# A decoder's first self-attention on one core: VectorE scales queries and keys in one operation, ScalarE spreads the keys

## The chip, the cores and the metric

The kernel runs on one core of a Trainium2 chip. The metric is the device time of one execution, in microseconds. Five instruction streams run side by side and meet only at semaphores: PE (TensorE), DVE (VectorE), ACT (ScalarE), POOL (GpSimd) and SP (SyncE, which here only issues transfers). An engine runs its own instructions strictly in the order in which they are written; a wait holds everything behind it on that engine.

## The reference, cut to what matters

Two decoder layers, each of attention, cross-attention and a feed-forward part with a layer norm after each, over 32 sequences of 64 tokens with 256 features. The change lies in the first attention alone:

```python
q = (x @ Wq + bq).reshape(B, T, N_HEAD, hd)      # 16 heads of 16
k = (x @ Wk + bk).reshape(B, T, N_GROUPS, hd)    # 4 groups of 16
v = (x @ Wv + bv).reshape(B, T, N_GROUPS, hd)
k = jnp.repeat(k, KV_PER_HEAD, axis=1)           # each group serves 4 heads
v = jnp.repeat(v, KV_PER_HEAD, axis=1)
q_hat = q / (norm(q) + EPS)
k_hat = k / (norm(k) + EPS)
q_r = apply_rope(q_hat * alpha * sqrt(hd), cos, sin)
k_r = apply_rope(k_hat, cos, sin)
attn = softmax(where(causal, q_r @ k_r.T / sqrt(hd), -inf))
return (attn @ v) @ Wo + bo
```

A length is taken of each of the 16 query heads and 4 key groups of a token, so there are 20 lengths to a token; a key group's result is needed four times.

## The kernel before

**Tiles and slots.** The 2048 tokens are 16 tiles of 128 (two sequences each). The self-attention is a pipeline written out by hand as a loop over 21 slots, once for each engine. In slot s the engines work on different tiles: the projection of tile s, the rotation and the turning of queries and keys of tile s-1, scores and softmax of tile s-2, the weights' transposes and the mix with the values of tile s-3, the output projection of tile s-4, sums and norm of tiles s-5 and s-6. What runs beside it: ScalarE and GpSimd cut the context into bf16 parts for the cross-attention that follows (`cast`, `remainder`), and SP loads and stores them.

**The tile's way.** `project` (PE, L593 to L600) writes queries, keys and values of a tile to PSUM (`a_qkv`). `projected` (ACT) writes the squares to `sq` (L402), the values to `qk` (L403) and V to `vbd` (L409 twice). `squares` (DVE, L476) sums the squares of 20 heads, `norms` (POOL, L351 and L353) takes roots. `rotate` (DVE, L489 to L502) rotates, takes the reciprocal of the lengths, multiplies it by the heads' factors, and scales: L500 the 16 query heads (256 elements in a partition), L502 the 4 key groups, each written four times (256 elements again), both into `qkr`. `turn_queries_keys` (PE, L665) transposes the 32 blocks of `qkr` in four matmuls into `a_tr`, which waits for both scalings (`rotated`). `queries_keys` (ACT, L428 and four times L431) copies them out, then come `scores` (PE, L613, L619), `softmax` (DVE, L466, L470), `exps` (ACT, L421), `weights` (PE, L630), `weights_out` (ACT, L395), `mix` (PE, L640), `quotient` (DVE, L510, L514), `turn_y` (PE, L649), `y_turned_out` (ACT, L415), `output` (PE, L655, L658), `sums` (DVE, L521 to L527) and `apply` (DVE, L481).

**Names of tiles.** Several buffers are parts of one allocation and appear in the profile by the name of that: `qk`, `sq`, `turned`, `rot`, `qkr` and the context's rows are all `a_front`; `qT`, `kbd`, `sm` are `a_middle`; `pr`, `pt` are `a_late`; `vbd`, `yT`, `yn` are `a_rest`. All but `vbd` have two buffers, taken by the tile's parity.

**The order in a slot**, which no planner changes. PE: `project(s)`, `weights(s-3)`, `scores(s-2)`, `turn_y(s-4)`, `turn_queries_keys(s-1)`, `mix(s-3)`, `output(s-4)`. ACT: `projected(s)`, `weights_out(s-3)`, `cast(s,1)`, `y_turned_out(s-4)`, `queries_keys(s-1)`, `exps(s-2)`, `cast(s,2)`, `cast(s+1,0)`. DVE: `rotate(s-1)`, `squares(s)`, `apply(s-6)`, `sums(s-5)`, `softmax(s-2)`, `quotient(s-3)`. POOL: `remainder(s,0)`, `norms(s)`, `remainder(s,1)`, `variance_power(s-5)`. `projected(t)` waits for the matmuls of `project(t)`, and `project(t)` for the copies out of `a_qkv` that `projected(t-1)` makes. The cross-attention starts behind the last tiles (its first scores on PE are L1059).

Of the kernel before, what the change touches and what calls it, by code (L numbers as in the profile page):

```python
# [20 lines left out]
ALU = mybir.AluOpType  # L21
ACT = mybir.ActivationFunctionType
# [39 lines left out]
class Kernel:  # L62
# [23 lines left out]
    def sem(self, name):  # L86
        self.sems.append(self.nc.alloc_semaphore(name=name))
        return self.sems[-1]
# [142 lines left out]
def self_attention(k, ctx):  # L231
# [44 lines left out]
    first_in, x_in = sem("a_first_in"), [sem(f"a_x_in{c}") for c in range(NCHUNK)]  # L276
    c_loaded, c_written = ([sem(f"a_{n}{v}") for v in range(3)] for n in ("context_in", "parts_written"))
    FILLS, filled = 13, sem("a_rows_filled")
    bo_full, bo_out, bo_steps, bo_split = sem("a_bo_full"), sem("a_bo_out"), sem("a_bo_steps"), sem("a_bo_split")
    qkv_full, sq_out, qk_out, v_out = sem("a_qkv_full"), sem("a_sq_out"), sem("a_qk_out"), sem("a_v_out")  # L280
    summed, normed, rot_steps, rotated = sem("a_summed"), sem("a_normed"), sem("a_rot_steps"), sem("a_rotated")
    qk_turned, qT_out, kbd_out = sem("a_qk_turned"), sem("a_qT_out"), sem("a_kbd_out")
    s_full, max_done, shifted, exped = sem("a_s_full"), sem("a_max_done"), sem("a_shifted"), sem("a_exped")
    pt_full, pt_out, y_full, rc_done, y_out = sem("a_pt_full"), sem("a_pt_out"), sem("a_y_full"), sem("a_rc_done"), sem("a_y_out")
# [10 lines left out]
    def live(t):  # L295
        return 0 <= t < TILES
# [81 lines left out]
    def scalar(act, between):  # L378
        for dst, src in consts:
            act.dma_start(dst[:], io[src]).then_inc(const, 16)  # L380

        def cast(t, j):
            if j == 0:
                act.wait_ge(c_loaded[t % 3], 16 * (t // 3 + 1))
                if t >= 3:
                    act.wait_ge(c_written[t % 3], 48 * (t // 3))
            else:
                act.wait_ge(c_left, 2 * t + j)
            act.activation(c_parts[t % 3][:, j, :], c_in[t % 3][:], ACT.Copy).then_inc(split if j == 2 else c_cast, 1)

        def weights_out(t):
            act.wait_ge(pt_full, t + 1)
            if t >= 2:
                act.wait_ge(y_full, t - 1)
            act.activation(pt[t % 2][:], pt_ps[:], ACT.Copy).then_inc(pt_out, 1)  # L395

        def projected(t):
            act.wait_ge(qkv_full, t + 1)
            if t >= 2:
                act.wait_ge(rotated, 2 * (t - 1))  # L400
            flat = qkv_ps[:, 0:NQK].rearrange("p (h d) -> p h d", d=HD)
            act.activation(sq[t % 2][:], flat, ACT.Square).then_inc(sq_out, 1)  # L402
            act.activation(qk[t % 2][:], flat, ACT.Copy).then_inc(qk_out, 1)  # L403
            v4 = qkv_ps[:, NQK:NQK + 2 * NV].rearrange("p (b g d) -> p b g d", b=2, g=GROUPS)
            if t >= 4:
                act.wait_ge(y_full, t - 3)
            for h2 in range(2):
                rows = slice(h2 * T, (h2 + 1) * T)
                act.activation(vbd[t % 4][rows, :, :, h2, 0:HD], v4[rows], ACT.Copy).then_inc(v_out, 1)  # L409

        def y_turned_out(t):
            act.wait_ge(y_turned, t + 1)
            if t >= 2:
                act.wait_ge(o_full, t - 1)
            act.activation(yT[t % 2][:], o_tr, ACT.Copy).then_inc(yT_out, 1)  # L415

        def exps(t):
            act.wait_ge(shifted, t + 1)
            if t >= 2:
                act.wait_ge(pt_full, t - 1)  # L420
            act.activation(pr[t % 2][:].rearrange("p a b -> p (a b)"), sm[t % 2][:].rearrange("p a b -> p (a b)"),  # L421
                           ACT.Exp).then_inc(exped, 1)

        def queries_keys(t):
            act.wait_ge(qk_turned, t + 1)
            if t >= 2:
                act.wait_ge(s_full, t - 1)
            act.activation(qT[t % 2][:], tr[:, 0:2, :], ACT.Copy).then_inc(qT_out, 1)  # L428
            kT = tr[:, 2:4, :].rearrange("p h (b s) -> p (h b) s", b=2)
            for j in range(4):  # L430
                act.activation(kbd[t % 2][:, :, j, :], kT, ACT.Copy, scale=k.headmask[:, j:j + 1]).then_inc(kbd_out, 1)  # L431

        cast(0, 0)
        for s in range(SLOTS):
            if live(s):
                if s == 0:
                    act.wait_ge(vbd_set, 12)
                projected(s)
            if live(s - 3):
                weights_out(s - 3)  # L440
            if live(s):
                cast(s, 1)
            if live(s - 4):
                y_turned_out(s - 4)
            if s == 1:
                act.wait_ge(bo_full, 1)
                act.wait_ge(bias_done, 1)
                act.activation(bo_rows, o_ps[0:3, :], ACT.Copy).then_inc(bo_out, 1)
            if live(s - 1):
                if s == 1:  # L450
                    act.wait_ge(const, 16 * len(consts))
                queries_keys(s - 1)
            if live(s - 2):
                exps(s - 2)
            if live(s):
                cast(s, 2)
            if live(s + 1):
                cast(s + 1, 0)
            between(act, s)

    def vector(dve, between):
# [21 lines left out]
        def rotate(t):  # L483
# [6 lines left out]
            for a in range(2):  # L490
# [6 lines left out]
            dve.wait_ge(rot_steps, n + 4)  # L497
            dve.tensor_tensor(sc[v][:], sc[v][:], factor[:], ALU.mult).then_inc(rot_steps, 1)
            dve.wait_ge(rot_steps, n + 6)
            dve.tensor_tensor(qkr[v][:, 0:HEADS, :], rot[v][:, 0:HEADS, :], sc[v][:, 0:HEADS].unsqueeze(2).broadcast_to([P, HEADS, HD]),  # L500
                              ALU.mult).then_inc(rotated, 1)
            dve.tensor_tensor(qkr[v][:, HEADS:2 * HEADS, :].rearrange("p (g j) d -> p g j d", j=4),  # L502
                              rot[v][:, HEADS:H20, :].unsqueeze(2).broadcast_to([P, GROUPS, 4, HD]),
                              sc[v][:, HEADS:H20].unsqueeze(2).unsqueeze(3).broadcast_to([P, GROUPS, 4, HD]), ALU.mult).then_inc(rotated, 1)

        def quotient(t):
            v = t % 2
# [19 lines left out]
            dve.bn_aggr(mv[v][:], stats[v][:]).then_inc(mv_done, 1)  # L527

        def split_output_bias():
            dve.wait_ge(bo_out, 1)  # L530
            for j in range(3):
                if j:
                    dve.wait_ge(bo_steps, 2 * j)
# [49 lines left out]
    def tensor(pe, between):  # L583
# [74 lines left out]
            pe.matmul(o_ps, k.onesb[0:3, :], bo3[:], start=False, stop=True).then_inc(o_full, 1)  # L658

        def turn_queries_keys(t):  # L660
            pe.wait_ge(rotated, 2 * (t + 1))
            if t >= 1:
                pe.wait_ge(kbd_out, 4 * t)
            for c in range(4):
                ins = pe.transpose(tr[:, c, :], qkr[t % 2][:, 8 * c:8 * c + 8, :].rearrange("p h d -> p (h d)"), k.ident[:])  # L665
            ins.then_inc(qk_turned, 1)

        pe.wait_ge(k.built, BUILT)
# [1 line left out]
        for s in range(SLOTS):  # L670
# [6 lines left out]
            if s == 1:  # L677
                pe.wait_ge(const, 16 * len(consts))
                pe.matmul(o_ps, k.ones[0:1, :], borow[:], start=True, stop=False)
                for c in range(KD):  # L680
                    ins = pe.matmul(o_ps, bvcol[:, c:c + 1].broadcast_to([P, P]), wo[:, c, :], start=False, stop=(c == KD - 1))
                ins.then_inc(bo_full, 1)
            if live(s - 4):
                turn_y(s - 4)
            if live(s - 1):
# [2832 lines left out]
```

## Time and profile before

| | us |
|---|---|
| median of three runs | 1169.81 |
| the runs | 1169.81, 1172.21, 1169.0 |
| the profiled execution, its device time | 1168.21 |
| its span in the trace | 1166.2 |
| PE busy in the span | 1075.0 |
| DVE busy | 782.5 |
| ACT busy | 601.0 |
| POOL busy | 474.0 |

The span is the time from the first to the last instruction in the trace; the device time is 2.0 us more. The self-attention takes up the first 150 us of the span or so. Its slots are no part of the page's chain that ended last, which was followed back only to 602 us; what bounds them is read from the timelines of the engines. The idle time of an engine ahead of an instruction stands behind its row in square brackets, with what ended it.

### The profile page before, as it was taken

The numbers are of one execution on the slowest core, as the hardware profiler recorded it, in microseconds if no ns is written. First come the engines' busy times: TensorE is split into PE (matmuls) and PEld (weight loads), VectorE is DVE, ScalarE is ACT, GpSimd is POOL, SyncE is SP. The second block draws the span as 40 slices with busy tenths as digits, with TensorE's granted clock in tenths as the row PEclk, the third lists the DMA queues.
The fourth block names the chain that finished last, engine by engine and source line by source line (L and its number), as shares of the span: only waits on it lengthen the run. The fifth ranks groups of instructions, "written<-read, shape, count | busy, mean of one in ns | idle before, by whom it ended". The sixth has DMA issues, their size and how long they took to land. (4 is left out here: it accounts for less than half of the span.)

```text
span 1166.2 us, 20808 instructions
## 1 busy us (share of the span) xinstructions
PE 1075.0 (92%) x7240; PEld 650.8 (56%) x7240; DVE 782.5 (67%) x1500; ACT 601.0 (52%) x1260; POOL 474.0 (41%) x820
## 2 busy tenths in 40 slices
PE   6999999999998796999978899999998999999998
PEld 3676675555554343677533455577775434545455
DVE  4999977888886331333396686889997565564655
ACT  2888747777778511333268555458874332121210
POOL 5887745666665264233235254564331000000001
PEclk9999999999999998999989999999999999999999
DMA  5976466565652222264323000112000000000000
GB/s 188 311 220 201 121 189 160 146 150 153 155 151 75 82 82 82 71 179 130 116 84 122 15 1 1 38 46 56 11 15 16 1 0 1 10 9 10 10 8 29
DMA packets 82459, 100.36 MB, mean 86 GB/s; under 512 B 13715, under 2 KB 69165, under 8 KB 81677
## 3 DMA queue, kind: packets, MB, share of 16 engines
q1 hardware_dynamic: 74915, 85.97, 26.1%
q0 software_dynamic: 3408, 9.34, 2.3%
q10 hardware_dynamic: 4034, 3.72, 1.0%
q8 instruction: 60, 0.98, 0.4%
q14 instruction: 42, 0.34, 0.1%
HBM read 59.83 MB, written 33.36 MB: 80 GB/s over the span
## 5 line engine op out<-in xcount | busy, mean ns | idle before, releaser
L2892 POOL TENSOR_SCALAR f_rstd<-f_mv 128x1 f32<-128x1 f32 x16 | 3.8, 235 | 251.9 <-DVE f_mv L3044 251.8
L942 DVE TENSOR_REDUCE b_nm<-a_s 128x4 f32<-128x1024 f32 x64 | 78.1, 1221 | 33.6 <-PE a_s L1059 32.2
L2989 DVE TENSOR_TENSOR f_prod<-f_sg,f_kept 128x512 f32<-128x512 f32 (+1 forms) x48 | 33.2, 692 | 96.5 <-ACT f_kept L2920 92.5
L1006 ACT ACTIVATE a_late<-a_qkv 128x512 f32<-128x512 f32 x128 | 76.3, 596 | 40.0 <-PE a_qkv L1119 39.4
L3132 PE MATMUL cps_h<-residT,w_f_w 128*128 128x512 f32 x176 | 82.4, 608 | 3.4 <-DVE f_inner L3026 1.9
L2914 ACT ACTIVATE f_sg<-cps_h 128x512 f32<-128x512 f32 (+1 forms) x24 | 14.3, 596 | 125.3 <-PE cps_h L3151 109.3
L942 DVE TENSOR_REDUCE b_nm<-a_pt 128x4 f32<-128x1024 f32 x64 | 77.0, 1204 | 2.0 <-PE a_pt L1059 2.0
L1006 ACT ACTIVATE a_late<-a_y 128x512 f32<-128x512 f32 x128 | 76.3, 596 | 1.9
L1134 PE MATMUL a_o<-a_late,b_vt 128*32 128x256 f32 x1024 | 68.4, 385 | 5.8 <-ACT a_late L1006 5.8
L1451 POOL DMA_INDIRECT routed<-c_out,c_target x39 | 37.3, 957 | 82.4 <-ACT c_out L1533 82.1
L351 POOL TENSOR_TENSOR a_nrm<-a_ss,phalf 128x20 f32<-128x20 f32 x16 | 58.0, 3622 | 17.2 <-DVE a_ss L476 16.9
L2131 DVE SCALAR_TENSOR_TENSOR d_acc<-d_pad,d_cw,d_acc 128x512 f32<-128x512 f32 x72 | 58.0, 811 | 2.8 <-ACT d_acc L2030 1.1
L1659 DVE TENSOR_TENSOR c_hid<-c_sg,cps_h 128x176 f32<-128x176 f32 x39 | 13.2, 338 | 64.2 <-issue 50.6
L3132 PEld LDWEIGHTS cps_h<-residT,w_f_w 128*128 128x128 f32 x176 | 32.8, 191 | 39.8 <-issue 33.7
L1721 PE MATMUL cps_h<-c_wgu,c_xT 128*128 x156 | 52.8, 461 | 0.7 <-ACT c_xT L1521 0.7
L2262 PE MATMUL cps_h<-residT,d_win 128*128 128x512 f32 x96 | 46.9, 619 | 0.8 <-ACT residT L1494 0.5
L1949 POOL TENSOR_TENSOR d_rs<-d_ms,mhalf 128x4 f32<-128x4 f32 x16 | 22.7, 1420 | 61.2 <-DVE d_ms L2188 61.2
L2914 ACT ACTIVATE f_sg<-f_kept 128x512 f32<-128x512 f32 (+1 forms) x24 | 15.2, 632 | 58.1 <-DVE f_kept L2994 58.1
L1134 PEld LDWEIGHTS a_o<-a_late,b_vt 128*32 128x32 f32 x1024 | 27.6, 109 | 30.4 <-issue 11.0
L1560 DVE TENSOR_TENSOR c_hid_s<-c_sg_s,cps_t 128x512 f32<-128x512 f32 (+1 forms) x12 | 8.2, 686 | 51.1 <-ACT c_sg_s L1484 25.8
L1445 POOL DMA_INDIRECT xrows<-c_xr,c_place_int x32 | 31.1, 972 | 27.6 <-DVE c_xr L1628 18.2
L1740 PE MATMUL cps_o<-c_wd,c_hT 88*128 x156 | 40.1, 380 | 0.0
(445 smaller groups left out, 2923.7 us busy)
## 6 DMA issues: line engine op xcount, KB each, us to landing
kparts<-a_rest SPq DMA_DIRECT2D x48, 192.0 KB, 4.0
a_rest<-a_rest SPq DMA_DIRECT2D x64, 128.0 KB, 3.1
xrows<-in_c_fill SPq DMA_DIRECT2D x13, 387.0 KB, 4.4
c_xrow<-xrows SPq DMA_DIRECT2D x39, 129.0 KB
c_back<-routed SPq DMA_DIRECT2D x16, 256.0 KB, 3.4
a_front<-kparts SPq DMA_DIRECT2D x12, 288.0 KB
a_front<-qparts SPq DMA_DIRECT2D x36, 96.0 KB
qparts<-b_xp SPq DMA_DIRECT2D x48, 64.0 KB, 3.3
```

Of the source, the lines that this page charges most:

```text
L351: gp.tensor_tensor(nrm[v][:], ss[v][:], k.phalf[:, 0:H20], ALU.pow).then_inc(normed, 1)
L942: dve.tensor_reduce(nm[s % 2][:, 4 * n:4 * n + 4].rearrange("p (g h) -> p g h", h=2), s1[step % 2][:], AX.X, ALU.max, negate=True).then_in ...
L1006: act.activation(pr[g % 8][:], s2[g % 2][:], ACT.Exp, scale=SCALE).then_inc(s2_out, 1)
L1134: ins = pe.matmul(o_ps[32 * j:32 * j + 32, q % 2, :], vt[x % 2][:, lh, g, :], pr[g % 8][:, lh, :], start=(lh == 0), stop=(lh == KD - 1))
L1445: gp.indirect_dma_start(k.xrows[:], bass.IndirectOffsetOnAxis(ap=place_int[n][:, t:t + 1], axis=0), xr[:, t, :], None).then_inc(scattered[ ...
L1451: gp.indirect_dma_start(routed[:], bass.IndirectOffsetOnAxis(ap=target[s % 8][:], axis=0), out[s % 4][:], None).then_inc(sent[s % 4], 16)
L1721: ins = pe.matmul(h_ps[s % 2][:, 0:2 * F], xT[s % 2][:, kd, :], wgu[:, kd, ds(e, 1), :].rearrange("p a f -> p (a f)"), start=(kd == 0), st ...
L1740: ins = pe.matmul(o_ps[:, s % 2, 0:D], hT[s % 2][:, c, :], wd2[:, ds(e, 1), c, :].rearrange("p a f -> p (a f)"), start=(c == 0), stop=(c = ...
L2131: ins = dve.scalar_tensor_tensor(out=acc[v][:], in0=pad[v][:, :, tap:tap + T], scalar=cw[:, m, tap:tap + 1], in1=acc[v][:], op0=ALU.mult, ...
L2262: ins = pe.matmul(bank[:], win[:, kd, m * P:(m + 1) * P] if m < XT else wz[:, kd, (m - XT) * P:(m - XT + 1) * P], k.residT[:, kd, c * CHUN ...
L2989: dve.tensor_tensor(prod[n % 2][at], sg[n % 2][at], up, ALU.mult).then_inc(prod_done, 1)
L3132: pe.matmul(h_ps[j][:], (w1, w3)[j][:, kd, m * P:(m + 1) * P], k.residT[:, kd, c * CHUNK:(c + 1) * CHUNK], start=(kd == 0), stop=False)
```

## The change

Three things are edited, all in `self_attention`.

1. `rotate`: L500 and L502 become one operation, which scales the 20 heads and groups (320 elements) into the first 20 blocks of `qkr`. `rotated` rises by one for a tile instead of two.
2. ACT gets a new instruction `spread_keys`: it copies the four key groups of `qkr`, each four times (256 elements in a partition), into the first 16 blocks of `sq`, the buffer of the squares, which `squares` has read by then. It stands behind `cast(s,1)` and ahead of `y_turned_out(s-4)`, waits for `rotated` and raises `keys_spread`.
3. `turn_queries_keys` waits for `keys_spread` too, and takes its third and fourth block from `sq`. `projected` waits in addition for the turning of the tile that had its buffers before.

To have a semaphore for this, `bo_full` and `bo_out` (used once, in slot 1) become one that counts to two.

```diff
@@ projected (ACT)
             if t >= 2:
-                act.wait_ge(rotated, 2 * (t - 1))
+                act.wait_ge(rotated, t - 1)
+                act.wait_ge(qk_turned, t - 1)
@@ new (ACT)
+        def spread_keys(t):
+            act.wait_ge(rotated, t + 1)
+            act.activation(sq[t % 2][:, 0:HEADS, :].rearrange("p (g j) d -> p g j d", j=4),
+                           qkr[t % 2][:, HEADS:H20, :].unsqueeze(2).broadcast_to([P, GROUPS, 4, HD]), ACT.Copy).then_inc(keys_spread, 1)
@@ the slot's order (ACT)
             if live(s):
                 cast(s, 1)
+            if live(s - 1):
+                spread_keys(s - 1)
             if live(s - 4):
                 y_turned_out(s - 4)
@@ rotate (DVE)
-            dve.tensor_tensor(qkr[v][:, 0:HEADS, :], rot[v][:, 0:HEADS, :], sc[v][:, 0:HEADS].unsqueeze(2).broadcast_to([P, HEADS, HD]),
-                              ALU.mult).then_inc(rotated, 1)
-            dve.tensor_tensor(qkr[v][:, HEADS:2 * HEADS, :].rearrange("p (g j) d -> p g j d", j=4),
-                              rot[v][:, HEADS:H20, :].unsqueeze(2).broadcast_to([P, GROUPS, 4, HD]),
-                              sc[v][:, HEADS:H20].unsqueeze(2).unsqueeze(3).broadcast_to([P, GROUPS, 4, HD]), ALU.mult).then_inc(rotated, 1)
+            dve.tensor_tensor(qkr[v][:, 0:H20, :], rot[v][:], sc[v][:].unsqueeze(2).broadcast_to(full), ALU.mult).then_inc(rotated, 1)
@@ turn_queries_keys (PE)
-            pe.wait_ge(rotated, 2 * (t + 1))
+            pe.wait_ge(rotated, t + 1)
+            pe.wait_ge(keys_spread, t + 1)
             if t >= 1:
                 pe.wait_ge(kbd_out, 4 * t)
             for c in range(4):
-                ins = pe.transpose(tr[:, c, :], qkr[t % 2][:, 8 * c:8 * c + 8, :].rearrange("p h d -> p (h d)"), k.ident[:])
+                half = (qkr if c < 2 else sq)[t % 2][:, 8 * (c % 2):8 * (c % 2) + 8, :]
+                ins = pe.transpose(tr[:, c, :], half.rearrange("p h d -> p (h d)"), k.ident[:])
```

ACT's instructions of one slot in the middle of the self-attention, from the squares' copy to the next slot's first cast, before the change; the names behind "waits" are semaphores:

```order
L402 ACTIVATE a_front<-a_qkv 128x320 [waits a_rotated,a_qkv_full]
L403 ACTIVATE a_front<-a_qkv 128x320
L409 ACTIVATE a_rest<-a_qkv 64x8x16 [waits a_y_full]
L409 ACTIVATE a_rest<-a_qkv 64x8x16
L395 ACTIVATE a_late<-a_pt 128x1024 [waits a_y_full,a_pt_full]
L389 ACTIVATE a_rest<-a_front 128x256 [waits a_context_left]
L415 ACTIVATE a_rest<-a_o 128x256 [waits a_o_full,a_y_turned]
L428 ACTIVATE a_middle<-a_tr 128x256 [waits a_s_full,a_qk_turned]
L431 ACTIVATE a_middle<-a_tr,headmask 128x4x64 x4
L421 ACTIVATE a_late<-a_middle 128x1024 [waits a_pt_full,a_shifted]
L389 ACTIVATE a_rest<-a_front 128x256 [waits a_context_left]
L389 ACTIVATE a_rest<-a_front 128x256 [waits a_parts_written0,a_context_in0]
```

The same slot on ACT with the change, as far as the line that is numbered L415 there (the new copy) and what follows it:

```order
L404 ACTIVATE a_front<-a_qkv 128x320 [waits a_qk_turned,a_rotated,a_qkv_full]
L405 ACTIVATE a_front<-a_qkv 128x320
L411 ACTIVATE a_rest<-a_qkv 64x8x16 [waits a_y_full]
L411 ACTIVATE a_rest<-a_qkv 64x8x16
L396 ACTIVATE a_late<-a_pt 128x1024 [waits a_y_full,a_pt_full]
L390 ACTIVATE a_rest<-a_front 128x256 [waits a_context_left]
L415 ACTIVATE a_front<-a_front 128x256 [waits a_rotated]
L422 ACTIVATE a_rest<-a_o 128x256 [waits a_o_full,a_y_turned]
L435 ACTIVATE a_middle<-a_tr 128x256 [waits a_s_full,a_qk_turned]
L438 ACTIVATE a_middle<-a_tr,headmask 128x4x64 x4
```

One instruction is new, behind the projection's copies, the weights' copy and a cast, and ahead of both copies that PE's later work waits for.

PE's instructions from the end of the scores to the mix in such a slot, with the change (before it, the first turning of queries and keys waits for `a_kbd_out` and `a_rotated` alone):

```order
L624 MATMUL a_s<-a_middle 64x256 x8
L654 MATMUL a_o<-ident,a_rest 128x128 [waits a_o_out,a_y_out]
L654 MATMUL a_o<-ident,a_rest 128x128
L672 MATMUL a_tr<-ident,a_front 128x128 [waits a_kbd_out,a_keys_spread,a_rotated]
L672 MATMUL a_tr<-ident,a_front 128x128 x3
L645 MATMUL a_y<-a_rest,a_late 64x34 [waits a_y_out,a_pt_out]
L645 MATMUL a_y<-a_rest,a_late 64x34 x15
```

Nothing moves on PE; the turning has one wait more, and the mix, the output and the next projection are queued behind it.

## Rows read from the trace of the kernel before

**Rows 1.** Stretches: start:end, length, busy us of PE, PEld, DVE, ACT, POOL; clock, DMA.
```profile
52.00:60.00 8.00, 8.00 (x114) 5.82 (x110) 7.79 (x19) 6.72 (x17) 6.44 (x7) 1.00 1.06 347
92.00:100.00 8.00, 7.69 (x94) 5.47 (x93) 7.83 (x18) 6.59 (x16) 6.45 (x7) 1.00 0.60 187
...
150.00:160.00 10.00, 10.00 (x74) 7.80 (x71) 8.55 (x16) 2.10 (x6) 2.30 (x6) 1.00 0.75 203
```

**Rows 2.** Timeline of DVE, slot 12: start us, duration us, engine, line, operation.
```profile
103.51 0.42 DVE L500 TENSOR_TENSOR a_front<-a_front,a_sc 128x256 f32<-128x256 f32 x1
...
104.19 0.48 DVE L476 TENSOR_REDUCE a_ss<-a_front 128x20 f32<-128x320 f32 x1
```

**Rows 3.** Timeline of PE, slots 11 and 12.
```profile
97.77 0.60 PE L665 MATMUL a_tr<-ident,a_front 128*128 128x128 f32 x4
...
99.35 1.13 PE L655 MATMUL a_o<-a_rest 128*128 128x256 f32 x4
...
100.62 1.34 PE L593 MATMUL a_qkv<-a_rest,residT 128*128 128x320 f32 x4
...
102.14 0.73 PE L600 MATMUL a_qkv<-a_rest,residT 128*64 128x64 f32 x16
...
105.47 0.41 PE L649 MATMUL a_o<-ident,a_rest 128*128 128x128 f32 x2 [0.32 <-DVE a_rest L521]
105.72 0.60 PE L665 MATMUL a_tr<-ident,a_front 128*128 128x128 f32 x4
```

**Rows 4.** Timeline of ACT, slots 11 and 12.
```profile
98.40 0.38 ACT L428 ACTIVATE a_middle<-a_tr 128x256 f32<-128x256 f32 x1
...
100.45 1.06 ACT L421 ACTIVATE a_late<-a_middle 128x1024 f32<-128x1024 f32 x1 [0.21 <-DVE a_middle L470]
101.58 0.72 ACT L389 ACTIVATE a_rest<-a_front 128x256 bf16<-128x256 f32 x2
102.91 0.44 ACT L402 ACTIVATE a_front<-a_qkv 128x320 f32<-128x320 f32 x1 [0.60 <-PE a_qkv L600]
...
105.07 0.41 ACT L389 ACTIVATE a_rest<-a_front 128x256 bf16<-128x256 f32 x1
```

**Rows 5.** Operation L489 on DVE, alone and beside L358 of POOL: two timelines.
```profile
39.30 0.48 DVE L489 TENSOR_TENSOR a_front<-a_front,a_cos 128x320 f32<-128x320 f32 x1
```
```profile
100.96 0.94 DVE L489 TENSOR_TENSOR a_front<-a_front,a_cos 128x320 f32<-128x320 f32 x1
```
```profile
100.88 0.67 POOL L358 TENSOR_TENSOR a_front<-a_front,a_rest 128x256 f32<-128x256 f32 x1
```

**Rows 6.** ACT's groups up to 150 us: busy us, mean ns | idle before.
```profile
L389 ACT ACTIVATE a_rest<-a_front 128x256 bf16<-128x256 f32 x48 | 18.4, 410 | 19.7 <-POOL a_front L358 14.5 <-DMA a_front<-in_ctx_dg 3.4 <-DMA kparts<-a_rest 1.1
```

**Rows 7.** Timelines of ACT and PE in slot 3: two hand-overs to a waiting PE.
```profile
36.41 1.02 ACT L395 ACTIVATE a_late<-a_pt 128x1024 f32<-128x1024 f32 x1
```
```profile
35.81 0.66 PE L665 MATMUL a_tr<-ident,a_front 128*128 128x128 f32 x4
37.49 1.13 PE L640 MATMUL a_y<-a_rest,a_late 128*64 128x34 f32 x32 [1.03 <-ACT a_late L395]
```

**Rows 8.** Timeline of ACT: the squares' copies (L402) of slots 3, 5 and 15.
```profile
35.18 0.42 ACT L402 ACTIVATE a_front<-a_qkv 128x320 f32<-128x320 f32 x1
...
48.50 0.44 ACT L402 ACTIVATE a_front<-a_qkv 128x320 f32<-128x320 f32 x1
```
```profile
126.76 0.44 ACT L402 ACTIVATE a_front<-a_qkv 128x320 f32<-128x320 f32 x1 [0.60 <-PE a_qkv L600]
```

**Rows 9.** Timelines of ACT and PE behind the last projection.
```profile
134.50 1.02 ACT L395 ACTIVATE a_late<-a_pt 128x1024 f32<-128x1024 f32 x1 [0.70 <-PE a_pt L630]
```
```profile
133.37 1.09 PE L630 MATMUL a_pt<-ident,a_late 128*128 128x128 f32 x8 [0.87 <-ACT a_late L421]
...
136.62 0.60 PE L665 MATMUL a_tr<-ident,a_front 128*128 128x128 f32 x4
```
```profile
150.45 0.61 PE L1059 MATMUL a_s<-a_front 72*128 72x256 bf16 x4
```

More of the change, by code:

```diff
@@ L278, in self_attention @@
     FILLS, filled = 13, sem("a_rows_filled")
-    bo_full, bo_out, bo_steps, bo_split = sem("a_bo_full"), sem("a_bo_out"), sem("a_bo_steps"), sem("a_bo_split")
+    bo_rows_made, bo_steps, bo_split = sem("a_bo_rows_made"), sem("a_bo_steps"), sem("a_bo_split")
     qkv_full, sq_out, qk_out, v_out = sem("a_qkv_full"), sem("a_sq_out"), sem("a_qk_out"), sem("a_v_out")
     summed, normed, rot_steps, rotated = sem("a_summed"), sem("a_normed"), sem("a_rot_steps"), sem("a_rotated")
+    keys_spread = sem("a_keys_spread")
     qk_turned, qT_out, kbd_out = sem("a_qk_turned"), sem("a_qT_out"), sem("a_kbd_out")
@@ L445, in scalar @@
             if s == 1:
-                act.wait_ge(bo_full, 1)
+                act.wait_ge(bo_rows_made, 1)
                 act.wait_ge(bias_done, 1)
-                act.activation(bo_rows, o_ps[0:3, :], ACT.Copy).then_inc(bo_out, 1)
+                act.activation(bo_rows, o_ps[0:3, :], ACT.Copy).then_inc(bo_rows_made, 1)
             if live(s - 1):
@@ L529, in split_output_bias @@
         def split_output_bias():
-            dve.wait_ge(bo_out, 1)
+            dve.wait_ge(bo_rows_made, 2)
             for j in range(3):
@@ L681, in tensor @@
                     ins = pe.matmul(o_ps, bvcol[:, c:c + 1].broadcast_to([P, P]), wo[:, c, :], start=False, stop=(c == KD - 1))
-                ins.then_inc(bo_full, 1)
+                ins.then_inc(bo_rows_made, 1)
             if live(s - 4):
```

## The prediction, made before the changed kernel was run

> **What bounds the kernel now.** Only the self-attention changes, so I read its slots and leave the rest of the program alone. The page's chain of what ended last doesn't reach back that far, so the order of views is: busy time by stretches, then the timelines of DVE, PE and ACT over one slot.
>
> The stretches show two regimes [rows 1]. In 52 to 60 us PE is busy all 8.00 us. In 92 to 100 us DVE is busy 7.83 us and PE 7.69. The timelines then show who waits for whom. A slot lasts 7.95 us (the turning L665 starts at 97.77 and at 105.72) [rows 3]. In it PE waits once, 0.32 us ahead of L649, for DVE's L521 [rows 3]. So PE alone would need 7.95 - 0.32 = 7.63 us, and DVE, which has hardly an idle moment (7.83 of 8 us), sets 7.95 [rows 1]. ACT is busy 6.59 us of 8 [rows 1] and waits 0.60 us ahead of L402 for the projection and 0.21 ahead of L421 [rows 4]. By busy time the change looks right: it takes work from the full engine and gives it to one with room.
>
> What matters is where the work is put. ACT's new copy stands between the projection's copies and PE's turning of queries and keys, and PE's next projection is queued behind that turning. That makes a loop which isn't there now, and I price it.
>
> **DVE: one operation for two.** L500 starts at 103.51 and L476, behind L502, at 104.19: the two take 0.68 us [rows 2]. The merged operation has 320 elements and a broadcast operand; the nearest row is L489 of the same size, 0.48 us alone [rows 5], of which about 0.08 overlaps with the next (0.42 us rows follow each other 0.34 apart). That is 0.40 us, a saving of 0.28 a slot, and DVE's own pace becomes 7.67. Its upper bound is an operation that meets GpSimd: L489 takes 0.94 us where L358 of POOL runs beside it (100.88 to 101.55) [rows 5]. With 0.46 us more, DVE would need 8.13 us and save nothing.
>
> Two timelines bear on this, and the Trainium skill (SBUF — State Buffer, "Who interferes with whom") says it as a rule: a VectorE operation with two SBUF inputs and a GpSimd operation that reads SBUF exclude each other, and the later one waits until the first is done. The trace agrees with it at L489. By that rule the merged operation is one candidate to be blocked where there were two.
>
> **ACT: the copy.** From L402 (102.91) to the cast L389 (105.07) are 2.16 us of unbroken work; the next instruction can start 0.31 us later (two casts take 0.72 us, one 0.41) [rows 4]. So the copy starts 2.47 us behind L402. Its length: L389 also reads 256 elements from SBUF and writes SBUF, 0.41 us mean over 48 [rows 6]; the lower bound is 0.38, L428 from PSUM [rows 4]; the upper bound 0.48, L489's on DVE, if the repeated read costs something. I take 0.41. The hand-over to a waiting PE takes 0.06 us: L395 ends at 37.43, L640 starts at 37.49 [rows 7]. DVE's result isn't late for the copy: L502 starts before 104.19, while the copy would start at 105.38 [rows 2, 4].
>
> **PE: from the turning to the next L402.** From L665 (97.77) to L402 (102.91) are 5.14 us with PE busy throughout: turning, mix, output, projection, and 0.04 us from L600's end to ACT [rows 3, 4]. When PE has waited, the four transposes take 0.66 instead of 0.60 us (L665 at 35.81) [rows 3, 7], so 5.20.
>
> **The new loop** is 2.47 + 0.41 + 0.06 + 5.20 = 8.14 us a slot. By the bounds of the copy it is 8.11 to 8.21. It is longer than DVE's 7.67 and PE's 7.63, so it decides: PE, which now could turn at 105.72, turns at 102.91 + 2.94 = 105.85 at best and starts cold, and DVE's saving has nowhere to go. ACT's own work (its copies, exps and casts) fits: copying out starts 0.71 us behind the turning (0.66 and the hand-over), L428's start to L421's end takes 2.8 us (98.40 to 101.51 less 0.21 idle, less an overlap of 0.1), two casts 0.63 more, so ACT is ready 4.2 us behind the turning, and L402 comes at 5.20 [rows 4].
>
> **Summed over the slots.** Up to slot 3 nothing is lost: ACT's casts wait for GpSimd's remainder there (five waits, 14.5 us in all [rows 6]), and L402 of slot 3 stays at 35.18 [rows 8]. From it on:
> - slot 3: the copy ends at 35.18 + 2.47 + 0.41, PE turns at 38.12 instead of 35.81 [rows 7]. The output isn't in this slot yet (1.27 us of PE, L655 to L593 [rows 3]), so L402 of slot 4 comes at 38.12 + 5.20 - 1.27 = 42.05; ACT itself needs until 42.1, which I take.
> - slot 4: L402 of slot 5 comes at 42.1 + 8.14 = 50.24 instead of 48.50 [rows 8].
> - slots 5 to 14: ten loops, 50.24 + 81.4 = 131.64 instead of 126.76 [rows 8]: 4.9 us later. Before, these ten took 78.26 us.
> - the end: slot 16 has no projection. PE turns tile 14 at 131.64 + 2.94 = 134.58; copying out and exps end 0.71 + 2.8 later, at 138.1; the weights' transposes take 1.13 until L395 can start (133.37 to 134.50) [rows 9], so it starts at 139.3. It runs 0.92 us until the next can start (no cast here), the copy 0.41, the hand-over 0.06: the last turning comes at 140.7 instead of 136.62 [rows 9]. So 0.8 us come back, and 4.1 are left.
>
> What follows (the cross-attention from 150.45 on [rows 9]) takes this tile's results and moves as a whole, since PE is busy without a gap from there (10.00 of 10 us [rows 1]). The span goes from 1166.2 to 1170.3 and the profiled execution's time from 1168.21 to 1172.3. The median of the runs is 1.6 us above the profiled one; I add 4.1 to it and forecast **1173.9 us**.
>
> Edits at no cost: `projected` waits for a turning that ACT has already waited for one slot earlier; the one semaphore instead of two in slot 1 changes no order; in slot 1 PE turns later by the casts and the copy (about 1.5 us), but ACT waits there for GpSimd, and without that cover it would cost the 1.5.
>
> **Rivals.**
> - *DVE's saving arrives (not slower).* If the copy were hidden, the slots bound by DVE (7 to 15, eight of them) would go at 7.67 instead of 7.95: 8 x 0.28 = 2.2 us less, 1167.6. It decides if the copy is done by the time that PE comes to the turning of its own accord, 2.5 us behind L402. For it speaks DVE's share [rows 1]; against it that ACT is only at the start of the copy then [rows 4]. The Trainium skill (Perfetto Trace Analysis, "Identifying the Most-Contended Engine") has the rule that stands behind this rival: optimise first the engine with the highest occupancy. The trace so far agrees that DVE is fullest, but not that it would stay so.
> - *The early slots absorb it.* If slots 4 to 7 lost nothing (waits for transfers or GpSimd that I don't see in them as binding), only eight slots would go from 7.95 to 8.14: 1.5 us, 1171.3.
> - *DVE pays too.* If the merged operation or its neighbours run into L358 once more a slot (0.46), DVE needs 8.13 and, since its maximum then starts late for the exps, DVE and ACT push each other: I set 0.25 us more for 10 slots, 1176.4.
> - *The copy is cheaper than it looks.* If it could start and end as soon as the cast (0.31 in all, not 0.47), the loop would be 7.98, and the sum 4.1 - 11 x 0.16 = 2.3 us: 1172.1.
>
> **How the numbers follow.** Forecast (a loss of 2.8 to 5.5 us) 0.64; cheap copy 0.10; early slots absorb it 0.10; DVE pays too 0.09; the saving arrives 0.07. The range reaches from the cheap copy and a part of the absorbed case to the case of the pushing engines: 1170.8 to 1176.8. About 0.3%, 3.5 us, is what a measurement of this kernel can tell from no change. Slower by more: 0.7 of the forecast's 0.64 and the 0.09, and a little of the rest, 0.56. Faster by more: 0.03, since even the arriving saving gives 2.2 us. Within: 0.41.
>
> **What would show it.** Right: slots 5 to 14 of 8.1 us; an idle entry ahead of the turning that names ACT's new copy; PE's wait for L521 gone; DVE with idle entries (about 0.5 us a slot) ahead of the maximum or the squares; the copy at 0.41 us; L402 of slot 15 near 131.6 and the cross-attention's first scores near 154.6. Wrong: slots of 7.7 us without a wait ahead of the turning, or a copy waiting for `rotated`, or idle entries elsewhere.

## The result and the profile after

Ten timed runs of each kernel, side by side on one chip, gave a median of 1178.01 us for the changed kernel (1173.01 to 1179.6) and 1171.43 us for the one before (1168.35 to 1178.73). The ratio is 1.005, with a 95% interval of 1.0031 to 1.007, that is 5.9 us slower (3.6 to 8.2); the medians themselves lie 6.6 us apart. The forecast was 1173.9 us in a range of 1170.8 to 1176.8, so the time lies 1.2 us above the range. The profiled execution took 1178.23 us, its span 1176.4 us.

The steady slots first. This is ACT's timeline over slot 11 of the changed kernel, with start, duration, engine, line and, in brackets, the idle time ahead; L404 is the squares' copy, L415 the new copy of the keys, L435 the first copy out of the turning:

```profile
102.29 0.44 ACT L404 ACTIVATE a_front<-a_qkv 128x320 f32<-128x320 f32 x1 [1.10 <-PE a_qkv L605]
...
104.46 0.41 ACT L390 ACTIVATE a_rest<-a_front 128x256 bf16<-128x256 f32 x1
104.77 0.41 ACT L415 ACTIVATE a_front<-a_front 128x256 f32<-128x256 f32 x1
105.07 0.38 ACT L422 ACTIVATE a_rest<-a_o 128x256 f32<-128x256 f32 x1
105.94 0.39 ACT L435 ACTIVATE a_middle<-a_tr 128x256 f32<-128x256 f32 x1 [0.49 <-PE a_tr L672]
...
110.44 0.44 ACT L404 ACTIVATE a_front<-a_qkv 128x320 f32<-128x320 f32 x1 [1.11 <-PE a_qkv L605]
```

PE in the same slot, and DVE and POOL ahead of it:

```profile
104.47 0.44 PE L654 MATMUL a_o<-ident,a_rest 128*128 128x128 f32 x2
105.27 0.63 PE L672 MATMUL a_tr<-ident,a_front 128*128 128x128 f32 x4 [0.36 <-issue]
```
```profile
101.39 0.89 DVE L509 TENSOR_TENSOR a_front<-a_front,a_sc 128x320 f32<-128x320 f32 x1
102.76 0.49 DVE L485 TENSOR_REDUCE a_ss<-a_front 128x20 f32<-128x320 f32 x1 [0.48 <-ACT a_front L404]
```
```profile
101.27 0.67 POOL L359 TENSOR_TENSOR a_front<-a_front,a_rest 128x256 f32<-128x256 f32 x1
```

The slot lasts 8.15 us (102.29 to 110.44) instead of 7.95. The copy starts 2.48 us behind L404, takes 0.41 and is done at 105.18; PE starts the turning at 105.27. The idle entry ahead of it is put down to "issue", but its end fits only the copy's. (In slot 1 the same entry is put down to L415.) The wait of PE for DVE's sums that stood in [rows 3] is gone, and DVE idles, as L485's entry shows, though its merged operation L509 ran into GpSimd's L359 and took 0.89 us (0.89 to 0.97 in every slot from the fifth on).

Then slots 3 and 4. These are the squares' copies of slots 3, 4, 5 and 15 on ACT, to be held against [rows 8]:

```profile
35.51 0.42 ACT L404 ACTIVATE a_front<-a_qkv 128x320 f32<-128x320 f32 x1
...
45.27 0.44 ACT L404 ACTIVATE a_front<-a_qkv 128x320 f32<-128x320 f32 x1 [2.29 <-PE a_qkv L605]
...
53.41 0.44 ACT L404 ACTIVATE a_front<-a_qkv 128x320 f32<-128x320 f32 x1 [1.11 <-PE a_qkv L605]
...
134.88 0.44 ACT L404 ACTIVATE a_front<-a_qkv 128x320 f32<-128x320 f32 x1 [1.11 <-PE a_qkv L605]
```

From 53.41 to 134.88 are ten slots of 8.147 us. But slot 4 begins at 45.27, where 42.1 was forecast: 3.2 us are lost in one slot. PE's timeline there, and PE's busy time and granted clock by stretches (the columns are those of [rows 1]; the clock is the number ahead of the DMA share):

```profile
35.02 1.09 PE L624 MATMUL a_s<-a_middle 64*64 64x256 f32 x16
38.47 1.08 PE L672 MATMUL a_tr<-ident,a_front 128*128 128x128 f32 x4 [2.35 <-issue]
39.48 1.93 PE L645 MATMUL a_y<-a_rest,a_late 128*64 128x34 f32 x32
41.34 2.50 PE L598 MATMUL a_qkv<-a_rest,residT 128*128 128x320 f32 x4
43.77 0.44 PE L601 MATMUL a_qkv<-a_bias,onesb 3*128 3x320 bf16 x1
44.14 1.09 PE L605 MATMUL a_qkv<-a_rest,residT 128*64 128x64 f32 x16
```
```profile
28.00:36.00 8.00, 6.25 (x77) 4.16 (x74) 6.98 (x16) 5.84 (x16) 5.53 (x5) 1.00 0.52 158
36.00:40.00 4.00, 1.65 (x18) 1.23 (x16) 2.80 (x3) 2.73 (x8) 3.83 (x2) 0.77 0.96 295
40.00:45.00 5.00, 5.00 (x48) 3.39 (x45) 3.17 (x9) 2.98 (x7) 1.69 (x4) 0.50 0.96 313
45.00:50.00 5.00, 4.64 (x73) 3.50 (x71) 2.88 (x4) 4.19 (x12) 3.61 (x2) 1.00 1.16 381
```

PE stands still from 36.11 to 38.47 us, because the turning waits for the copy. The granted clock falls from 1.00 to 0.50, the lower of TensorE's two levels (1.2 GHz), and the turning, the mix and the projection of tile 4 run at it: L645 takes 1.93 us and not 1.13, L598 2.50 and not 1.34. The loop from L404 of slot 3 to that of slot 4 is 9.76 us; forecast were 6.9. The rest of the 3.2 us, 0.33, was there when slot 3 began.

Where the time went, by landmarks of the two profiled executions:

| us | before | after | later by | forecast |
|---|---|---|---|---|
| squares' copy, slot 3 | 35.18 | 35.51 | 0.3 | 0 |
| slot 4 | 41.58 | 45.27 | 3.7 | 0.5 |
| slot 5 | 48.50 | 53.41 | 4.9 | 1.7 |
| slot 15 | 126.76 | 134.88 | 8.1 | 4.9 |
| cross-attention's first scores | 150.45 | 157.74 | 7.3 | 4.1 |
| span | 1166.2 | 1176.4 | 10.2 | 4.1 |

So 4.1 us are the loop, as forecast, 3.2 are lost by slot 4 beyond the forecast (2.9 by the clock, 0.3 before slot 3), and 2.9 come in behind the cross-attention.

### The profile page after: what moved, and what is told of

Read it like the earlier page. It is cut to its first block, busy times and chain, and to the rows that moved or that the text cites. A ratio compares the mean times of both kernels' runs of the same rounds, so it can differ in the third digit from the quotient of the medians.

```text
span 1176.4 us, 20809 instructions
## 1 busy us (share of the span) xinstructions
PE 1082.8 (92%) x7240; PEld 654.5 (56%) x7240; DVE 779.1 (66%) x1484; ACT 602.5 (51%) x1276; POOL 470.6 (40%) x820
## 4 chain that ended last, share of the span: by engine, by line
PE 40%; issue 10%; DVE 5%; ACT 5%; POOL 4%; DMA 2%; SPq 0%; POOLq 0%; ACTq 0%; DVEq 0%
PE cps_h L3139 7%; PE cps_h L2269 3%; POOL routed L1458 3%; PE cps_h L3158 3%; PE cps_t L2334 2%; PE cps_x L3172 2%; PE cps_o L1707 2%; PE cps_o L3197 2%; PE cps_h L2768 2%; PE cps_x L3197 2%; PE cps_t L3158 1%; PE cps_o L3158 1%; PE cps_h L1695 1%; ACT e_kbd L2579 1%; PE cps_t L1695 1%
## 5 line engine op out<-in xcount | busy, mean ns | idle before, releaser
L2269 PE MATMUL cps_h<-residT,d_win 128*128 128x512 f32 x96 | 45.3, 601 | 0.8 <-ACT residT L1501 0.5
```

Of the source, the lines that this page charges most:

```text
L2269: ins = pe.matmul(bank[:], win[:, kd, m * P:(m + 1) * P] if m < XT else wz[:, kd, (m - XT) * P:(m - XT + 1) * P], k.residT[:, kd, c * CHUN ...
```

## The experiments

The runs were made on more than one chip. The kernel before has medians of 1155.6 to 1169.7 us in them, so a time is held only against the kernel before of the same comparison, and traces mostly up to the first scores of the cross-attention.

**The two kernels once more.** No edit.

> The kernel before once more, to see what one execution's trace varies by. Theory A (the changed kernel loses 7.3 us up to the cross-attention by its order, and the remaining 2.9 us of the profiled executions' difference of 10.2 are TensorE's clock in the router's stretch, which falls by chance for longer or shorter): slots of 7.95 us, L402 of slot 15 at 126.8 and the first scores of the cross-attention at 150.5 again; between 385 and 490 us the clock may differ, and the span with it by up to 3 us. Rival B (the 2.9 us belong to the change): the span is 1166.2 again within 0.5 us.

> The changed kernel once more. Theory A: TensorE's clock falls again in slot 3 behind 2.3 us of idle PE (L404 of slot 4 at 45.3, of slot 15 at 134.9, first scores of the cross-attention at 157.7), and the rest from there to the end lasts between 1015.7 us, as in the kernel before, and 1018.7. Rival C (the fall in slot 3 is chance): slot 4 begins at 42.1, slot 15 at 131.6, first scores at 154.6.

Before: slot 15 at 126.52, first scores at 150.2, span 1151.0. After: slot 3 at 34.43, slot 4 at 44.16, slot 15 at 133.75, first scores at 156.6, span 1160.3. The loop of slot 3 is 9.73 us again. The two differ by 6.4 us at the first scores and by 9.3 in the span, so 2.9 us come in later once more. Rival C falls: slot 4 comes at 44.16 and not at 42.1, and everything is about 1.1 us earlier than A said because slot 3 began earlier. Rival B's span of 1166.2 can't be judged here, as this chip gives the kernel before a span of 1151.0; the 2.9 us seen twice speak for B, and A's part on the rest of the program isn't borne out by this pair. More on it below.

**PE kept busy in the gap of slot 3.**

```diff
             pe.wait_ge(rotated, t + 1)
-            pe.wait_ge(keys_spread, t + 1)
             if t >= 1:
                 pe.wait_ge(kbd_out, 4 * t)
+            if t == 2:
+                for n in range(14):
+                    pe.transpose(tr[:, n % 2, :], qkr[t % 2][:, 8 * (n % 2):8 * (n % 2) + 8, :]..., k.ident[:])
+            pe.wait_ge(keys_spread, t + 1)
             for c in range(4):
```

> The changed kernel, with 14 additional transposes on PE in slot 3 ahead of the wait for the copied keys (their results are overwritten at once). They fill the 2.3 us in which PE stood still. Theory A (idle PE, and so half the clock, costs 3.2 us in slots 3 and 4): no fall of the clock, L404 of slot 4 at about 42.2 instead of 45.3 and of slot 15 at 131.7 instead of 134.9; slots 5 to 14 still 8.145 us; the time 3 us below the changed kernel's and 4 us above the kernel before. Rival D (the clock falls whatever PE does there, or the fall costs nothing that is not waited for anyway): slot 15 at 134.9 as before.

PE's timeline in slot 3; L671 are the additional transposes:

```profile
35.88 1.75 PE L671 MATMUL a_tr<-ident,a_front 128*128 128x128 f32 x14
38.21 0.66 PE L675 MATMUL a_tr<-ident,a_front 128*128 128x128 f32 x4 [0.58 <-ACT a_front L415]
38.80 1.13 PE L645 MATMUL a_y<-a_rest,a_late 128*64 128x34 f32 x32
39.85 1.34 PE L598 MATMUL a_qkv<-a_rest,residT 128*128 128x320 f32 x4
```

The idle entry, 0.58 us long, now names the copy, L415. The mix and the projection keep the full clock (1.13 and 1.34 us), and slot 4 begins at 42.17, where the forecast had it. The slots behind stay at 8.19 us, 0.04 more than without the filling: PE starts 0.14 us behind the copy's end there (102.37 to 102.51) and not 0.09. Slot 15 begins at 132.24, the first scores at 155.2. The ratio to the kernel before is 1.0023 (1.0007 to 1.0039), 2.7 us, against 1.005 (1.0031 to 1.007) and 1.0046 (1.0028 to 1.0064) without the filling. Rival D falls by the trace: useless work on an engine that only waits took 2.9 us out of slot 3. The times agree with that in direction, by some 3 us, but their intervals overlap.

**The gap in slot 3 alone, without the loop.** To the kernel of copy_unwaited (below, whose slots are those of the kernel before) one wait is added:

```diff
-                pe.wait_ge(keys_spread, min(t, 14))
+                pe.wait_ge(keys_spread, t + 1 if t == 2 else min(t, 14))
```

> The kernel of copy_unwaited (VectorE scales twice, ScalarE's copy is read by nobody), but in slot 3 alone PE waits for the copy before the turning, as the changed kernel does in every slot. That makes one gap of some 2.3 us on PE, and no other. Theory A (a gap of this length there brings the clock down, and it stays down for the projection behind it): clock 0.5 from 38 to 45 us, L403 (the squares' copy) of slot 4 at 45.2 instead of 41.6, and about 3.5 us of it still there at slot 15 less what PE's own pace of 7.6 us makes up against VectorE's 7.95 in slots 4 to 6: 128.5 to 130.5 instead of 126.8. The time 2 to 3.5 us above the kernel before. Rival H (the fall in the changed kernel needs its other, shorter gaps too): slot 4 at 42.1, slot 15 at 127.3 or earlier, the time within 1 us of the kernel before.

```profile
38.09 0.63 PE L677 MATMUL a_tr<-ident,a_front 128*128 128x128 f32 x4 [2.20 <-issue]
38.65 1.13 PE L649 MATMUL a_y<-a_rest,a_late 128*64 128x34 f32 x32
39.70 2.41 PE L602 MATMUL a_qkv<-a_rest,residT 128*128 128x320 f32 x4
42.04 0.44 PE L605 MATMUL a_qkv<-a_bias,onesb 3*128 3x320 bf16 x1
```

The clock falls, but some 1.7 us behind the end of the gap (L649 still takes 1.13 us, L602 then 2.41). Slot 4 begins at 43.53, between what A and H had said, 8.40 us behind slot 3. It is 6.38 in copy_unwaited, and 6.87 in after_fill, which has the wait and no fall; by an estimate from these, 0.5 us are the wait and 1.5 the clock. Slot 15 begins at 129.97 and the first scores come at 153.6, the first as A had it, both 3.4 us behind the kernel before (before_again) and 3.2 behind copy_unwaited. The ratio is 1.0031 (1.0017 to 1.0045), 3.6 us. One wait in one slot, in a kernel that is otherwise the old one, costs some two thirds of what the whole change costs.

**The copy without its waiter.** VectorE makes both scalings and PE turns them, as before the change; ScalarE makes the copy too (not for the last two tiles), and nobody reads it. Of the edit only PE's part is shown; ScalarE and VectorE also wait for old copies before they write over their buffers.

```diff
-            pe.wait_ge(rotated, t + 1)
-            pe.wait_ge(keys_spread, t + 1)
+            pe.wait_ge(rotated, 2 * (t + 1))
+            if t >= 1:
+                pe.wait_ge(keys_spread, min(t, 14))
...
-                half = (qkr if c < 2 else sq)[t % 2][:, 8 * (c % 2):8 * (c % 2) + 8, :]
+                half = qkr[t % 2][:, 8 * c:8 * c + 8, :]
```

> The order of the kernel before on VectorE (two scalings) and on PE (the turning takes all four blocks from where VectorE put them), but ScalarE also makes the new copy, at the same place as in the changed kernel, for tiles 0 to 13; nobody reads the copy, and PE waits for it only one tile later, when it is long done. Theory A (what costs is PE's wait, not ScalarE's time): slots 7 to 15 stay at 7.95 us, L404 of slot 15 stays within 0.5 us of 126.5, and the time stays within 1 us of the kernel before. Rival F (ScalarE has no room for 0.41 us more): slots of 8.1 us or more, slot 15 at 128 to 132.

```profile
105.50 0.41 PE L658 MATMUL a_o<-ident,a_rest 128*128 128x128 f32 x2 [0.32 <-DVE a_rest L530]
```

PE has its old wait for DVE's sums again, 0.32 us. From slot 8 on the slots last 7.95 us, slot 15 begins at 126.78, the first scores at 150.5. The ratio is 0.9997 (0.9975 to 1.002). ScalarE had room for the copy; F falls. (The clock fell in slot 2 of this execution, behind 1.88 us of idle PE; slot 3 still began at 34.86, against 35.18 and 34.65 in the two traces of the kernel before.)

**The copy twice.**

```diff
-            act.activation(sq... , qkr..., ACT.Copy).then_inc(keys_spread, 1)
+            for n in range(2):
+                if n:
+                    act.wait_ge(keys_spread, 2 * t + 1)
+                act.activation(sq... , qkr..., ACT.Copy).then_inc(keys_spread, 1)
...
-            pe.wait_ge(keys_spread, t + 1)
+            pe.wait_ge(keys_spread, 2 * (t + 1))
```

> The changed kernel with the copy made twice, the second waiting for the first, and PE waiting for both. Theory A: the loop grows by a whole copy and the hand-over, 0.41 + 0.06, and the slot from 8.145 to 8.6 us; L404 of slot 15 about 5 us later than the changed kernel's, near 139.5. Rival B (another wait sets the slot): it grows by less than 0.2 us.

```profile
102.12 0.44 ACT L404 ACTIVATE a_front<-a_qkv 128x320 f32<-128x320 f32 x1 [1.11 <-PE a_qkv L608]
...
104.60 0.85 ACT L418 ACTIVATE a_front<-a_front 128x256 f32<-128x256 f32 x2
...
110.72 0.44 ACT L404 ACTIVATE a_front<-a_qkv 128x320 f32<-128x320 f32 x1 [1.11 <-PE a_qkv L608]
```

A second copy with its wait lengthens the work between L404 and PE by 0.44 us (0.85 for both), and the slot from 8.147 to 8.60, by 0.45: what is put there arrives whole. Slot 15 begins at 136.50 and not at 139.5, since the ten slots from slot 5 on grew by 4.5 us, but slot 4 began at 41.98: in this execution the clock did not fall in slot 3, though PE's gap there was 2.28 us long. Rival B, another wait, falls. The time, of a single execution, was 1180.77 us against a median of 1169.74 of the kernel before.

**PE waits ahead of the third transpose only.**

```diff
             pe.wait_ge(rotated, t + 1)
-            pe.wait_ge(keys_spread, t + 1)
             if t >= 1:
                 pe.wait_ge(kbd_out, 4 * t)
             for c in range(4):
+                if c == 2:
+                    pe.wait_ge(keys_spread, t + 1)
```

> The changed kernel, but PE waits for the copied keys only ahead of the third of the four transposes; the first two, of the queries, go as soon as VectorE has scaled. Theory A: half of the turning (0.30 us) leaves the loop, and the slot becomes 8.145 - 0.30 = 7.84 us. In slot 3 the idle time of PE of 2.35 us is cut in two, into a piece of some 0.1 and one of 1.9 us; whether TensorE's clock still falls there is open. L404 of slot 15 at 129 to 132. Rival B: the slot stays above 8 us.

```profile
37.32 0.44 PE L673 MATMUL a_tr<-ident,a_front 128*128 128x128 f32 x2 [2.06 <-ACT a_front L415]
37.69 1.13 PE L645 MATMUL a_y<-a_rest,a_late 128*64 128x34 f32 x32
38.74 2.07 PE L598 MATMUL a_qkv<-a_rest,residT 128*128 128x320 f32 x4
```

The slot is 7.91 us; 0.23 leave the loop and not 0.30, as two transposes behind a wait take 0.44. In slot 3 the clock falls behind a gap of 2.06 us (L598 takes 2.07, slot 4 begins at 42.33, 7.92 us behind slot 3). Slot 15 begins at 129.33, the first scores at 152.2. The ratio is 1.0023 (0.9997 to 1.005), so the time can't be told from the kernel before. Rival B, a slot above 8 us, falls.

**The merged scaling alone.** The copy and its wait are left out; three of four heads get the wrong keys.

```diff
-            if live(s - 1):
-                spread_keys(s - 1)
...
-            pe.wait_ge(keys_spread, t + 1)
...
-                half = (qkr if c < 2 else sq)[t % 2][:, 8 * (c % 2):8 * (c % 2) + 8, :]
+                half = qkr[t % 2][:, (0, 8, 12, 12)[c]:(8, 16, 20, 20)[c], :]
```

> The changed kernel without the copy: VectorE scales the 20 heads and groups in one operation, ScalarE copies nothing, and PE turns the unspread keys twice instead of the spread ones. Left out: three of four heads get other groups' keys, so the output isn't the reference's, and which tokens go to which expert later may change; the self-attention's own time is to be read up to the cross-attention's first scores. Theory A: VectorE's saving of 0.28 us becomes visible, the slot is 7.67 us by VectorE or 7.6 by PE, early slots are as in the kernel before, L404 of slot 15 at 124.5. Rival G (the merged operation meets GpSimd's L359 and takes 0.89 us, as in the changed kernel's trace, so nothing is saved): slots of 7.9 us or more.

```profile
101.27 0.49 DVE L507 TENSOR_TENSOR a_front<-a_front,a_sc 128x320 f32<-128x320 f32 x1
101.68 0.48 DVE L483 TENSOR_REDUCE a_ss<-a_front 128x20 f32<-128x320 f32 x1
```

The merged operation is as priced: 0.49 us, and 0.41 from its start to the next, where two took 0.68. The slots are 7.59 us where PE sets them and 7.68 at the end, where VectorE does; slot 15 begins at 123.71, the first scores at 146.8, 3.6 us earlier than before. The ratio is 0.9971 (0.9949 to 0.9992). The saving is real, and rival G falls. In the changed kernel the same operation took 0.89 us beside L359 of GpSimd, and no one waited for it.

**The copy early.** The same copy, one place earlier on ScalarE:

```diff
             if live(s):
                 projected(s)
+            if live(s - 1):
+                spread_keys(s - 1)
             if live(s - 3):
                 weights_out(s - 3)
             if live(s):
                 cast(s, 1)
-            if live(s - 1):
-                spread_keys(s - 1)
```

> The changed kernel with the copy of the keys moved on ScalarE from behind the cast to directly behind the projection's copies, ahead of the weights' copy; nothing else changes. Theory A (the loop from L404 over the copy to PE's turning and back sets the slot): the copy starts 1.24 us behind L404 instead of 2.47, the turning no longer waits for it, and the slot is set by VectorE's 7.67 us or PE's 7.63, about 7.7 in all; L404 of slot 15 at about 124 to 126; the time 2 us below the kernel before and 8 us below the changed one. Rival E (the place of the copy is not it, the new waits or GpSimd meeting the merged operation are): slots stay above 7.9 us.

> The kernel of copy_early again: the copy directly behind the projection's copies. Theory A: 2 to 3 us below the kernel before and 8 to 9 below the changed one; L404 of slot 15 near 124.9. In the cross-attention's opening (170 to 190 us) TensorE's clock may fall or not, in the same order of instructions, for up to 7 us; theory A takes this for chance, so in this execution it can be absent. Rival I (the earlier start of the cross-attention brings the fall with it): the clock is at 0.5 to 0.6 there again, and the medians show nothing of the 8 us.

ACT and PE in the slot that begins at 101.87:

```profile
101.87 0.44 ACT L404 ACTIVATE a_front<-a_qkv 128x320 f32<-128x320 f32 x1 [0.65 <-PE a_qkv L605]
...
103.11 0.42 ACT L415 ACTIVATE a_front<-a_front 128x256 f32<-128x256 f32 x1
103.55 1.02 ACT L396 ACTIVATE a_late<-a_pt 128x1024 f32<-128x1024 f32 x1
```
```profile
104.12 0.41 PE L654 MATMUL a_o<-ident,a_rest 128*128 128x128 f32 x2
104.37 0.60 PE L672 MATMUL a_tr<-ident,a_front 128*128 128x128 f32 x4
```

The copy starts 1.24 us behind L404 and is done at 103.53; PE comes to the turning at 104.37 with no wait. The slots are 7.60 us, PE's own pace, and 7.68 in the last two. Slot 15 begins at 124.86 and 125.98 in the two executions, the first scores come at 148.2 and 149.1. The ratios to the kernel before are 0.9978 (0.996 to 0.9995) and 0.9985 (0.9969 to 1.0001), that is 2.5 and 1.7 us faster; both comparisons point the same way, but the second interval reaches 1. E falls. By the two ratios of one chip this version is 7 us faster than the changed kernel; against the one before it is faster by little, at the edge of what these runs can tell.

The first execution of copy_early was one of its slowest (1159.46 us; median 1153.82). Two stretches of it, against those of the second:

```profile
170.00:180.00 10.00, 9.79 (x57) 5.29 (x61) 5.66 (x5) 5.35 (x11) 1.23 (x7) 0.53 0.32 83
180.00:190.00 10.00, 10.00 (x77) 5.23 (x69) 4.58 (x4) 5.10 (x10) 4.61 (x11) 0.62 0.33 88
```
```profile
170.00:180.00 10.00, 9.40 (x100) 5.70 (x101) 8.20 (x8) 8.57 (x18) 3.10 (x13) 1.00 0.38 117
```

In the first the clock was at half in the cross-attention's opening, with the same instructions in the same order and idle entries of under half a microsecond, and the stretch from the first scores to their last took 222.2 us instead of 214.8. The fall came in after_fill and copy_unwaited too, and not in the other ten traces, so rival I falls: an execution has it or not.

**The changed kernel, beside copy_early_2.**

> The changed kernel again, timed beside the next kernel on one chip. Theory A: 5 to 7 us above the kernel before; slots of 8.145 us, slot 4 late by the clock.

The ratio is 1.0046 (1.0028 to 1.0064), 5.3 us. The slots are 8.147 us; slot 4 begins at 43.21, 8.44 us behind slot 3 and not 9.7, since the clock came back sooner. Slot 15 begins at 132.81, the first scores at 155.7.

## Why the prediction was right and wrong

**Right: the direction and the loop.** Slower was forecast, and slower it is. The slot was forecast at 8.14 us and is 8.15 in three executions. The copy starts 2.48 us behind the squares' copy (2.47), takes 0.41 (0.41), and PE starts 0.09 behind its end (0.06). Moving the copy alone gives 7.60, doubling it 8.60, taking PE's wait away 7.95. The end gives back 0.8 us (0.8).

**Right in size, with no effect: VectorE's saving.** 0.27 us a slot by merge_alone, forecast 0.28. It never reached the end, because the rival that VectorE's saving arrives needs the copy to be hidden, and of the kernels with the copy that was true only for copy_early. The condition of the rival that VectorE pays too did come about (0.89 us beside GpSimd's operation), but not its price: the slots are 8.15 us.

**Wrong: slot 3.** The step "PE turns at 38.12 instead of 35.81 ... L402 of slot 4 comes at 38.12 + 5.20 - 1.27" took PE's work at the full clock, though the same line made a gap of over 2 us ahead of it. That term was put at 0.5 us and measured 3.7, 3.1 and 2.2 in the three traces of the changed kernel, against the trace of the kernel before from the nearest runs. The loop of slot 3 took 9.76, 9.73 and 8.44 us, and 6.87 where PE was kept busy: 2.9, 2.9 and 1.6 us are the clock. after_fill shows it from the other side: without the gap the term is as forecast. None of the four rivals had the clock in it, and the only cold-start term of the sum was 0.06 us. A place where the clock falls like that stood in the trace of before, behind the cross-attention, unread; PE's timeline there and two stretches:

```profile
394.88 0.44 PE L1144 MATMUL a_tr<-ident,a_rest 128*128 128x128 f32 x2 [1.83 <-POOL a_rest L904]
397.34 3.30 PE L1764 MATMUL cps_h<-residT,c_wr 128*32 128x512 f32 x16 [2.02 <-PEq L1187]
```
```profile
392.00:396.00 4.00, 1.49 (x5) 0.39 (x3) 0.47 (x2) 0.98 (x2) 2.04 (x3) 1.00 0.34 131
396.00:400.00 4.00, 2.66 (x16) 0.68 (x16) 0.00 (x0) 0.00 (x0) 0.00 (x0) 0.59 0.34 101
```

Behind idle entries of 1.83 and 2.02 us, with 0.44 us of work between them, the clock goes from 1.00 to half. What half the clock costs stood in slot 1:

```profile
21.99 1.11 PE L665 MATMUL a_tr<-ident,a_front 128*128 128x128 f32 x4 [3.48 <-DVE a_front L502]
22.90 2.43 PE L593 MATMUL a_qkv<-a_rest,residT 128*128 128x320 f32 x4
```

The same four transposes take 1.11 us instead of the 0.60 of [rows 3], and the projection 2.43 instead of 1.34. The gap of 3.48 us isn't shown to be the cause there, since the program's first projection, L593 at 5.80, had taken 2.47 us already and L593 at 11.22 too. (The granted clock of these stretches is listed as 1.00, from 22 to 28 us as well; at the start of this trace the durations tell, and not that column.)

**Wrong: the base.** The forecast stood on a median of three runs, 1169.81. Over the ten of the comparison it is 1171.43. The sum of 4.1 us on that base would have been 1175.5; with the 1.6 to 2.9 us of the clock it comes to 1177.1 to 1178.4, and 1178.01 was measured. That the three runs of the base lay 1.6 us low was bad luck, and would not have left the range by itself; it took the clock for that.

**Open in part: 2.9 us behind the cross-attention.** The profiled pairs of both kernels differ by 2.9 us more in the span than at the first scores, twice. The timed medians don't show it: after_fill lies 5.0 us behind the kernel before at the first scores and 2.7 in time, merge_alone 3.6 ahead and 3.4, copy_early in its two comparisons 2.0 and 1.1 ahead and 2.5 and 1.7. From the end of the cross-attention to the end of the program the traces fall into two groups by chip: those where the kernel before takes near 1170 us lie within 4.1 us of each other (770.3 to 774.4), those where it takes near 1156 us within 3.1 (756.4 to 759.5), the two of the kernel before near the low ends, but copy_unwaited and copy_early there too (770.3 and 757.7).

The traces say where it lies. In before and after the cross-attention itself is equally long, and from L2262 (L2269 in the changed kernel) to the end are 574.8 and 574.7 us; between the two, in the router's stretch and behind it, lie 196.4 and 199.5. At the start of that stretch, behind the two idle entries shown above, the clock is at half for some 3 us in the two traces of before, in copy_unwaited and in copy_early, for 7 in gap_slot3 and after_fill, and for 10 in the other seven, all three of the changed kernel among them (0.57 from 402 to 412 us in after, against 0.83 from 395 to 405 in before). The length of that part goes the same way in each group: 195.2 and 196.4 against 198.4 to 199.5, and 181.2 and 182.7 against 183.2 and 184.0 to 184.3. merge_alone, without the copy and its wait, has the long kind (199.0), and copy_early has the short kind in one execution (182.7) and the long in the other (184.0; another chip, but the changed kernel's long kind is 184.3 and 184.0 on the same two). So neither the copy nor PE's wait for it is needed for this loss, and one kernel can have it or not. Why all three traces of the changed kernel have the long kind is not shown.

## What to carry to other kernels

When work is moved to an engine with room, look at who waits for it and what is queued behind that waiter: an instruction of 0.4 us between two engines made a loop longer than the busiest engine's pace, and the same instruction one place earlier made none. Ask of every new gap on PE of a microsecond or two whether the clock holds; an early slot that seems to have slack is where such a gap appears. And take as many runs of the base as the effect is small.

## What the runs showed of the hardware

TensorE's granted clock fell from full to half behind idle gaps of 2.06 to 2.35 us in slot 3 (split_wait, gap_slot3 and the three traces of the changed kernel) and of 1.88 and 1.99 us in slot 2 (copy_unwaited, gap_slot3): before the work resumed (after) or up to 1.9 us into it (split_wait). It came back after 3 to 7 us. The length of the gap alone doesn't decide: in copy_early_2 the clock fell behind gaps of 1.13 and 0.37 us, and it held behind 2.28 us in copy_twice and 2.08 us in slot 2 of before_again. In three of thirteen traces it fell near 170 to 180 us, where the longest idle entries ahead were 0.47 and 0.48 us, for 3 to 7 us of loss. The Trainium skill (TensorE: Matmul & The Clock Gate, "Part 1") says of the clock's rise at the start of a kernel that its point is run-variable, and these traces agree: the projection of slot 1 took 2.47 us in after and after_2 and 1.31 in after_again, which are the same kernel. So is the fall: that kernel began slot 4 8.4 us behind slot 3 in one execution and 9.7 in two.
